# Twelve sliding maxima moved into the dense stage, query and key casts moved among the slide masks, score products over 64 rows

## The reference, cut to what matters

```
scores = jnp.einsum('bqhd,bkhd->bhqk', q, k) * scale
scores = jnp.where(allowed[None, None], scores, -jnp.inf)   # t - 64 <= key <= t
attn = jax.nn.softmax(scores, axis=-1)
out = jnp.einsum('bhqk,bkhd->bqhd', attn, v)
...
A = jnp.einsum('bchf,bshf->bhcs', qb, kb) * causal
y = jnp.einsum('bhcs,bshd->bchd', A, vb) + jnp.einsum('bchf,bhfd->bchd', qb, kv)
```

## Time and profile before

| | us |
|---|---|
| median of 3 runs | 1283.01 |
| profiled execution, its own time | 1290.89 |
| its span, first to last instruction | 1289.1 |
| PE busy | 1165.4 (90%) |
| DVE busy | 865.2 (67%) |
| ACT busy | 743.5 (58%) |
| POOL busy | 649.6 (50%) |
| mean granted clock of TensorE | 0.965 |

### The profile page before, as it was taken

The page is one execution under the profiler, slowest core; times in us unless marked ns, Lnnn a source line. Parts: engine busy times, 40 slices in busy tenths (PEclk is TensorE's granted clock), DMA queues, the critical chain, the costliest instruction groups (busy, mean ns, idle before and its releaser), DMA issues.

```text
span 1289.1 us, 26679 instructions
## 1 busy us (share of the span) xinstructions
PE 1165.4 (90%) x9122; PEld 750.8 (58%) x9122; DVE 865.2 (67%) x3433; ACT 743.5 (58%) x1580; POOL 649.6 (50%) x846
## 2 busy tenths in 40 slices
PE   5989999999999899989998999899989867988997
PEld 2445754565457545754575457545764456884896
DVE  4066588658865885688658865786578755885563
ACT  2356367735773577457745774477546624557675
POOL 4475254535444454545454544454445436675577
PEclk9998999999999899999999999899989969999999
DMA  7601620162015301540154015401472016542233
GB/s 237 153 3 54 177 73 12 54 184 73 13 55 147 108 15 39 151 120 15 39 152 117 17 39 151 117 17 39 139 211 64 5 26 142 82 70 29 41 55 40
DMA packets 123961, 105.53 MB, mean 82 GB/s; under 512 B 15242, under 2 KB 118578, under 8 KB 123826
## 3 DMA queue, kind: packets, MB, share of 16 engines
q1 hardware_dynamic: 102162, 85.89, 24.7%
q0 software_dynamic: 13792, 9.54, 5.1%
q10 hardware_dynamic: 7872, 8.39, 1.9%
HBM read 58.59 MB, written 46.37 MB: 81 GB/s over the span
## 4 chain that ended last, share of the span: by engine, by line
PE 49%; DVE 21%; ACT 13%; issue 8%; POOL 6%; DMA 2%; DVEq 0%; SPq 0%; POOLq 0%; ACTq 0%
PE bank L700 14%; PE heads L765 11%; ACT probs L1117 8%; PE bank L679 6%; PE bank L707 6%; DVE xnT_s L1585 4%; DVE hrow L1585 4%; DVE hT_s L1585 3%; POOL out L1362 3%; PE bank L690 2%; PE bank L675 2%; DVE spare L1585 2%; PE bank L1050 2%; PE bank L684 1%; PE bank L815 1%
## 5 line engine op out<-in xcount | busy, mean ns | idle before, releaser
L1117 ACT ACTIVATE probs<-bank 128x512 f32<-128x512 f32 (+2 forms) x896 | 441.2, 582 | 176.6 <-PE bank L707 169.8
L1309 POOL TENSOR_SCALAR_AFFINE_SELECT probs<-probs 128x384 f32<-128x384 f32 x256 | 127.7, 521 | 242.1 <-ACT probs L1117 242.1
L765 PE MATMUL heads<-probs,V 128*18 128x192 f32 (+9 forms) x3072 | 194.6, 394 | 10.7 <-POOL probs L1312 4.6
L707 PE MATMUL bank<-K,Q 128*128 128x192 bf16 (+4 forms) x1024 | 199.2, 271 | 4.3 <-ACT probs L1117 0.2
L707 PE MATMUL bank<-Q,K 128*128 128x192 bf16 (+4 forms) x1024 | 175.0, 275 | 16.3 <-ACT probs L1117 7.0
L1362 POOL DMA_INDIRECT out<-h1T_s x78 | 123.2, 1580 | 60.3 <-ACT h1T_s L1270 37.4
L765 PEld LDWEIGHTS heads<-probs,V 128*9 128x9 f32 (+1 forms) x3072 | 78.2, 94 | 122.3 <-issue 85.4
L1262 ACT ACTIVATE h2T_s<-bank,h1T_s 128x128 f32<-128x128 f32 x312 | 89.2, 368 | 93.1 <-PE bank L1050 80.9
L707 PEld LDWEIGHTS bank<-Q,K 128*128 128x128 bf16 x1024 | 81.4, 99 | 87.5 <-ACT probs L1117 31.1
L707 PE MATMUL bank<-QM,K 128*128 128x512 bf16 (+3 forms) x512 | 121.5, 301 | 7.8 <-DVE gatesT_s L1545 1.4
L707 PEld LDWEIGHTS bank<-K,Q 128*128 128x128 bf16 x1024 | 85.2, 98 | 67.7 <-DVE mx_c L1585 14.3
(11 more groups left out here) (241 smaller groups left out, 2285.1 us busy)
## 6 DMA issues: line engine op xcount, KB each, us to landing
K<-slots_of_k SPq DMA_DIRECT2D x64, 256.0 KB, 4.2
Q<-slots_of_q SPq DMA_DIRECT2D x15, 1024.0 KB, 10.9
QM<-slots_of_qm SPq DMA_DIRECT2D x8, 1024.0 KB, 9.4
h1T_s<-sorted_rows SPq DMA_DIRECT2D x78, 65.0 KB
slots_of_q<-Q SPq DMA_DIRECT2D x8, 384.0 KB, 2.6
slots_of_k<-QM SPq DMA_DIRECT2D x8, 384.0 KB, 2.9
slots_of_qm<-Q SPq DMA_DIRECT2D x8, 384.0 KB, 2.6
slots_of_k<-Q SPq DMA_DIRECT2D x8, 384.0 KB
```

Of the source, the lines that this page charges most:

```text
L707: mm = pe.matmul(to[:, at:at + right.shape[1]], left, right, start=True, stop=True, skip_group_check=True)
L765: mm = pe.matmul(heads[ROWS * i:ROWS * i + n, P * j:P * j + widths[j]], V[:, j, g // 2, i, first:first + n], slot_of(kind, 2 * g + i // 2) ...
L1117: return act.activation(to, bank, func, scale=scale, bias=bias).then_inc(taken_sem(run, unit), 1)
L1309: pool.affine_select(out=three, in_=three, compare_op=ALU.is_ge, fill=0.0, base=0, pattern=[[0, 3], [1, P]], channel_multiplier=-1)
```

## The change

Four things are changed.

1. The first 12 of the 32 sliding maxima (EARLY) leave the pairs stage. They stand in the dense stage of the sequence before, at the places of EARLY_AT, with all 128 rows. Their masked scores, which nothing reads, are written back into the bank (`in_place`) and not to SBUF. The pairs stage begins with 6 sliding maxima beside 10 scores, then goes one score to one maximum.
2. All other score products take only the 64 rows of the head (`own`). The units are put in an order in which the head's half alternates from unit to unit, in groups of four heads (`tri_unit`, `slide_unit`, HALVES); masks and `weigh` follow the groups.
3. GpSimd makes the mid and low parts of q1 and k1 behind slide mask 3, and those of qm1 behind mask 5. On SP the fetches come as QM, lower K1, Q1, upper K1, the store of the result stands behind the sends, the load of x before them.
4. In the dense stage, h2_3 stands before the logits, `copy_heads(SLIDE, 1)` is on ScalarE and not on VectorE, and VectorE takes v1 later.

```diff
-AHEAD, LEAD = 12, 8
+EARLY, AHEAD, LEAD = 12, 6, 10
...
+SCORED = AHEAD + PAIRS + 10
...
+    return min(LEAD + (PAIRS + HALF - LEAD) * (d - AHEAD) // (SCORED - AHEAD), 2 * PAIRS)
...
+EARLY_AT = {"h1_1": (0, 2), "h1_2": (2, 4), "h1_3": (4, 5), "cols": (5, 7), "h2_0": (7, 8), "h2_1": (8, 10), "h2_2": (10, 12)}
...
+            def own(h):
+                return slice(SROWS * (h % SH), SROWS * (h % SH + 1))
...
             def tri_scores(run, units, keys, buf, n):
                 def part(h, j, at):
-                    return at, keys[:, h, P * j:P * (j + 1)], q_part(buf, h, P * j, TRI_N[j])
+                    return at, keys[own(h), h, P * j:P * (j + 1)], q_part(buf, h, P * j, TRI_N[j], own(h))
...
+            def early(run, behind):
+                for n in range(*EARLY_AT[behind]):
+                    if n == 0:
+                        wait_slide_slots((run[1], 1))
+                    slide_max(run, n)
...
+            def wait_slide_slots(sequence):
+                pe.wait_ge(S["slots_k1"], due("slots_k1", sequence, FETCHED))
+                pe.wait_ge(S["slots_q1"], due("slots_q1", sequence, 16))
...
                 if after:
+                    sp.wait_ge(S["sent_k1"], due("sent_k1", (b, 1), SENT))
+                    fetch_sent((b, 1), "qm1")
                     if this:
                         sp.wait_ge(taken_sem(run, SLIDE_UNITS[-1]), taken_at(run, SLIDE_UNITS[-1]))
                     if part == "opening":
                         sp.wait_ge(S["keys1_cleared"], 2)
-                    sp.wait_ge(S["sent_k1"], due("sent_k1", (b, 1), SENT))
                     fetch("k1", LOWER)
-                    fetch_sent((b, 1), "qm1")
+                    fetch_sent((b, 1), "q1")
                     fetch("k1", UPPER, "upper")
-                    fetch_sent((b, 1), "q1")
...
-                if after:
-                    split_rest(nxt, ("q1", "k1", "qm1"))
+                    if p == 3 and after:
+                        split_rest(nxt, ("q1", "k1"))
+                    if p == 5 and after:
+                        split_rest(nxt, ("qm1",))
...
-            def row_max(run, unit, parts):
+            def row_max(run, unit, parts, in_place=False):
                 dve.wait_ge(full_sem(run, unit), full_at(run, unit))
-                beside = masked[PLACE[run[0]][unit][0]]
+                beside = bank_of(run, unit) if in_place else masked[PLACE[run[0]][unit][0]]
```

More of the change, by code:

```diff
@@ L561, in body @@
                         send((b, 1), name, 0)
-                if before and this:
-                    store(run, b - 1)
                 if this and after:
@@ L566, in body @@
                 if after:
-                    for n in (1, 2):
-                        for name in ("q1", "k1", "qm1"):
-                            send((b, 1), name, n)
+                    for name, n in (("q1", 1), ("k1", 1), ("q1", 2), ("k1", 2), ("qm1", 1), ("qm1", 2)):
+                        send((b, 1), name, n)
+                if before and this:
+                    store(run, b - 1)
                 if not after:
@@ L962, in dense_stage @@
                     dense_low(run, "h1_1", layer1, 1)
+                    early(run, "h1_1")
                 weigh(now, SLIDE, 3)
@@ L965, in dense_stage @@
                     dense_low(run, "h1_2", layer1, 2)
+                    early(run, "h1_2")
                 turn_heads(run, now, SLIDE, 1)
@@ L979, in dense_stage @@
                     dense_low(run, "h2_1", layer2, 1)
+                    early(run, "h2_1")
                     dense_low(run, "h2_2", layer2, 2, range(9))
@@ L1906, in dense_stage, with early @@
                 low = this and after
+                def early(behind):
+                    for n in range(*EARLY_AT[behind]):
+                        slide_max(run, n)
+                if after and not this:
+                    take_v1(run)
                 if this:
@@ L1934, in dense_stage @@
                     normalize(now, 2, x1)
+                    if low:
+                        early("h2_2")
                     if not after:
@@ L2008, in _ @@
             dve.wait_ge(S["masks_ready"], 1)
+            for n in range(EARLY):
+                slide_max(("opening", -1), n)
             dve.wait_ge(S["later_weights"], 16 * LATER_LOADS)
```

192 lines of the change are left out of this document (116 added, 76 removed).

## The result

| | before | after |
|---|---|---|
| median of the runs | 1283.3 us (4) | 1501.9 us (4; 1496.1 to 1510.4) |
| span of the profiled execution | 1289.1 | 1494.4 |
| PE busy, share of the span | 90% | 81% (1207.7 us; before 1165.4) |
| mean granted clock of PE | 0.965 | 0.892 |
| a round (from one sum x1 on VectorE to the next, mean of 7) | 129.4 | 152.7 |

The ratio after to before is 1.171, with a 95% interval of 1.165 to 1.177. The change costs 219 us where 49 were forecast. Of the 205 us between the two spans, 7 rounds hold 7 x 23.3 = 163, the opening and the first round 39.5, the tail 3. PE was busy 42 us longer (1165.4 to 1207.7) and waited 163 us longer (123.7 to 286.7).

A forecast was written before the change was run, and what follows sets the result against it. PE was taken as nearly full in all stages, with VectorE soon stopping its gain in the pairs stage. Terms summed to +7.0 us a round, times 7 = +49: median 1332 us, own range 1295 to 1365, 8 in 10 1240 to 1375.

The forecast's parts named there:

- The new wait: Dense stage: PE waits behind h1_1 for lower K1 and Q1, held behind QM's fetch; +9.5 us a round, 0 to 11.5.
- The clock behind the wait: Dense stage: PE's wait drops its clock, so h1_2 runs about 6 us at half speed; +3 us a round, 0 to 4.
- The masks at the end of a group: Masks come in twos, at most one mask (2.0 us) later; `weigh` is four units behind, so hidden, no cost.
- passed over as ending on ScalarE: First round's pairs stage: no causal maxima and its end on ScalarE, so counted as 0.
- slide stage: Half of 4.8 us of scores saved on PE, less ScalarE's limit and 18 row changes; -0.6 us a round, -2 to +2.
- The pairs stage: PE's gain mostly lost in front of VectorE, the bound; 58.3 against 60.2 us, -1.9 a round, -9 to +4.
- a sign of being wrong: Pairs stage: VectorE idling over 10 us there would show the prediction wrong.
- rival B: Pairs stage: PE waits more, its clock falls and `weigh` slows; +5.5 us a round, 1371 us; chance 0.12.
- h2_3 before the logits: Dense stage: h2_3 fills PE's 2.41 us gap for xnT and avoids its slow run behind it; -4.8 us a round.
- The twelve maxima: Dense stage: twelve sliding maxima moved there cost PE 12 x 0.15 = +1.8 us a round; VectorE's 7.1 us hidden.
- Rival C: Pairs and slide stages: 64-row products run one after another, not together; +2.6 us a round, 1350 us; chance 0.14.
- the rule on draining: Slide stage: changing tiling mode drains the TensorE, so each change would cost 0.16 us and the stage +0.5.

The follow-up runs named there:

- e4: The kernel after with units, slots and masks in groups of two heads, the unit of both heads taking all rows; 1421.9 us.
- e1: The kernel after with its twelve early maxima later in the dense stage: six behind h2_0, four behind h2_1, two behind h2_2; 1433.9 us.
- e15: The kernel after with the fetch of QM on SP moved behind lower K1, Q1 and upper K1; 1468.3 us.
- e5: The kernel after with the power for the next sequence's norm moved ahead of causal mask 6 on GpSimd; 1478.2 us.
- e3: The kernel after with all 128 rows in every score product, in the same order; 1460.2 us.
- e8: The kernel before with h2_3 ahead of the logits and the Gelu of h2_2 first on ScalarE; 1280.3 us.
- e2: The kernel after with the Gelu of h2_2 on ScalarE moved right behind the copy of hT2; 1474.5 us.
- e7: The kernel of e6 with all 128 rows in every score product; 1303.2 us.
- e11: The kernel of e10 with all 128 rows in every score product; 1279.4 us.
- e10: The kernel after without early maxima, scores and maxima alternating as before, groups of two heads, Gelu of h2_2 first, still 64 rows; 1296.9 us.
- e6: The kernel after with the edits of e1, e2 and e4 together, scores still over 64 rows; 1322.9 us.

## Why the prediction was wrong

The sign and the largest term of the sum, the new wait, were right; the size, 49 for 219 us, was off by more than the range allowed. The step that failed with the most weight is one that was put at nothing: masks that come in twos at the end of a group of four heads, "so it is hidden". Groups of two gave back 80 us (e4). The next is the pairs stage, where VectorE was to be the bound with 5 us of idle time and had 17.5.

- **The new wait, +9.5: right.** 8.9 measured in the round shown, QM issued 5.8 us after the stage began (about 6 foretold), Q1 there after 19.6 us (18.3). e1: 68 us over 7 rounds and the first. The step's reason, that QM holds K1 and Q1 back, was a smaller part than thought (3.8 us, e15).
- **The clock behind the wait, +3: wrong place.** Only the `weigh` behind the wait is slow (2.42 us; before 1.38), +1; h1_2 runs at full speed, and e1 gave nothing back in the clock. The clock is low from 321.7 to 328.6, and for 4.0 of these 6.8 us PE stands in the wait. The loss through the clock is elsewhere and much larger, 93 us in all; in the round shown, 2.2 us of it are the first pieces of the dense stage.
- **The masks at the end of a group, 0: wrong, some 80 us (e4).** "`weigh` is four units behind, so it is hidden" looked at `weigh` in a steady round alone. In the first round, passed over as ending on ScalarE, each `weigh` waits 3.2 to 4.1 us for them, four times, and then runs at about half speed; up to the first x1 the kernel is 39.5 us longer, and e4 gave 19 back. In the **slide stage (-0.6: wrong, +3.0)** the power for the norm is behind mask 6 on the same queue, and that has no slack: 3.7 us of wait, gone in e5.
- **The pairs stage, -1.9: wrong, +7.2.** The sum had VectorE as the bound: 3.2 + 45.0 us of work and 5 of idle time, at most 8. Its work was about right (49.9), its idle time 17.5, over the 10 that the prediction had named as a sign of being wrong. PE was busy 58.3 us, not 43: only three in ten neighbouring score products overlap in the trace (590 of 2019 start early, counted at the full clock), and 5 us of the 58.3 are the lower clock (an estimate: half of the busy time in the three low stretches). That a PE which stops in front of VectorE runs its other work slower was put into rival B at 0.12. Some `weigh` of the steady rounds took 3.3 to 4.5 us for 2.35, the third layer 5.5 for 3.7. It was set aside there with one row, 2.52 of 4 us busy at 1.00: one stretch in which the clock held says little of a whole stage. Of the 10.2 us that pairs and slide stage grew by together, e4 gave back 8.6 and e3 3.8; the two overlap.
- **h2_3 before the logits, -4.8: right for its stage (-6.0 in e8), wrong for the round (-1.4).** The prediction counted the 3.2 us of VectorE at the start of the next stage as VectorE's; e8 shows it as a wait of PE, 2.6 us. In the kernel after, 1.3 us of the gain are also eaten by the low clock (356.49 to 360.63, 4.1 us for 2.85).
- **v2 and h2_2 share a bank, not foreseen: +3.4 a round, 27 us (e2).** The ring of banks stood in the code of the change; nobody followed it to ScalarE's queue.
- **The twelve maxima, +1.8 on PE: about right alone** but never repaid. With everything else mended and all rows (e7 against e11) they still cost 2.3 us a round and 7 before the first x1.
- **Rival C was wrong**: scores of a pair start 0.01 us apart. The price of a change of rows was about right: 0.10 us taken, 0.095 to 0.098 measured in e10, under the 0.16 that was worked out for the rule on draining. What had no term is that the pairs stage has such changes too.

In parts, by the medians: place of the maxima 68 (e1), bank 27 (e2), groups of four 80 (e4), together 179 by e6; halved rows another 20 (e7); the rest, to e11's 1279, the maxima themselves. That these places cost what they do is shown by the runs; that a clock which falls behind short waits is part of it rests on the windows and on e3.

## What to carry to other kernels

When one engine gets faster in front of a slower one, ask what it does behind its new waits: here the halved products saved PE some 50 us, and waits, changes of rows and a lower clock took more. When units are regrouped or inserted, walk every queue and every ring of buffers one turn further: who stands behind a wait that now ends later (the power behind a mask), and whose buffer the new seventh neighbour takes. A gain in one stage is a gain only when the engine that opens the next stage is ready too.

## What the runs showed of the hardware

- Products over 64 rows on alternating halves start 0.01 us apart (215.80 and 215.81), 512 columns each still lasting 0.37 to 0.39 us. PE's busy time in the two stages was no less for it in e10 (88.1 us; 87.6 in e11).
- A change between score products of 64 and of 128 rows costs 0.095 to 0.098 us each way (medians of e10's trace), so some 50 us in a kernel with 746 of them.
- PE's clock fell without long gaps. In the kernel after most waits of the pairs stage are under 1 us (the longest 2.9), and yet the stage's mean clock is 0.92; it fell at 246.63 after 4 us in which PE was counted as busy for 3.73. The Trainium skill (TensorE: Matmul & The Clock Gate, A second HAM failure mode: psum-queue depth-cycling) describes it: a PE that cycles through the banks of PSUM and idles briefly and often between groups moves between its two clocks. The traces agree that it does: 131 us lost to the clock after, against 38 before. No run here changes the short waits alone.
- Filling an idle stretch with work held the clock in it (1.00) but did not keep it up behind (0.57), and the transfer that was waited for took 2.0 us longer in that run.
